# Attention with 16 heads of width 8 on one Trainium2 core: two heads on the two row halves of TensorE, head stacks built through DRAM, maxima six pairs ahead

## The reference, cut to what matters

```python
Q, K, V = relu(xn @ Wq + bq), relu(xn @ Wk + bk), relu(xn @ Wv + bv)   # 16 heads, width 8
scores = Q K^T / sqrt(8)                    # per head, 512 x 512
scores = where(key_mask == 0, NEG, scores)  # key_mask: token's sum is not 0
scores = where(tril == 0, NEG, scores)      # causal
out = (softmax(scores) * query_mask) @ V + xn
s = gamma * (out - mean) / sqrt(var + 1e-8) + beta
x1 = x + s * g                              # g: gate from the feed-forward part
```

## Time and profile before

| | |
|---|---|
| median of 3 runs | 3548.79 us (3545.11 to 3551.12) |
| profiled execution | 3541.39 us |
| its span, first to last instruction | 3539.7 us |
| mean granted TensorE clock over the span | 0.933 |
| attention0, first score matmul of its first unit | 489.0 us |
| attention0, first score matmul of its last unit | 1415.4 us |
| start of attention1's first DMA | 1453.6 us |

### The profile page before, as it was taken

One profiled execution on the slowest core, in us unless ns is written; L12 is line 12 of the kernel. 1 busy time (PEld: TensorE's weight loads), 2 busy tenths in 40 slices (PEclk: granted clock), 3 DMA queues, 4 the chain that ended last, 5 costly groups with the idle time before them and its releaser, 6 DMA issues. The chain is left out here.

```text
span 3539.7 us, 67118 instructions
## 1 busy us (share of the span) xinstructions
PE 2813.7 (79%) x21299; PEld 1950.8 (55%) x21313; DVE 2355.2 (67%) x5836; ACT 1522.0 (43%) x2623; POOL 1306.7 (37%) x1528
## 2 busy tenths in 40 slices
PE   0035348777777777499999999999999986999999
PEld 0023224444444444266666666666666656888888
DVE  8977657777777777366666666666666645555555
ACT  3434325444444445245555555555555542232222
POOL 4557621212121211155555555555555550000000
PEclk9977669998998989699999999999999998999999
DMA  1000021322222221101111111111111102010010
GB/s 48 0 6 0 8 40 35 50 35 46 40 42 37 43 42 32 42 24 35 34 35 36 34 34 34 34 34 34 34 34 34 31 29 69 24 36 24 27 32 24
DMA packets 152526, 116.23 MB, mean 33 GB/s; under 512 B 35506, under 2 KB 127155, under 8 KB 152372
## 3 DMA queue, kind: packets, MB, share of 16 engines
q1 hardware_dynamic: 152372, 114.25, 14.0%
HBM read 60.96 MB, written 17.32 MB: 22 GB/s over the span
## 5 line engine op out<-in xcount | busy, mean ns | idle before, releaser
L1518 DVE CUSTOM_DVE_ANT_0 a_scored<-a_pMax,a_causal 128x128 bf16<-128x128 f32 (+3 forms) x1024 | 449.8, 485 | 446.1 <-PE a_pMax L1642 446.1
L927 DVE TENSOR_REDUCE a_max<-a_pMax 128x2 f32<-128x256 f32 (+3 forms) x512 | 406.9, 823 | 206.7 <-PE a_pMax L1063 198.4
L866 ACT ACTIVATE a_PT<-a_pST 128x512 f32<-128x512 f32 x640 | 370.7, 597 | 401.9 <-PE a_pST L603 264.9
L1435 ACT ACTIVATE a_PT<-a_pST 128x1024 f32<-128x1024 f32 (+1 forms) x384 | 339.2, 883 | 365.4 <-PE a_pST L1632 354.3
L1061 PE MATMUL a_pMax<-a_KS,a_QS 96*128 96x128 bf16 (+3 forms) x1024 | 283.6, 329 | 200.3 <-DMA a_QS<-a_mT 131.3
L1384 POOL TENSOR_SCALAR_AFFINE_SELECT a_PT<-a_PT 128x256 f32<-128x256 f32 x512 | 204.0, 411 | 607.0 <-ACT a_PT L1435 576.6
L1921 ACT ACTIVATE m_silu<-m_pG 128x512 f32<-128x512 f32 x256 | 153.3, 599 | 409.1 <-PE m_pG L2013 409.1
L1650 PE MATMUL a_pO<-a_PT,a_V 128*64 128x512 f32 (+3 forms) x2048 | 307.4, 443 | 0.7 <-POOL a_PT L1384 0.7
L1061 PEld LDWEIGHTS a_pMax<-a_KS,a_QS 96*128 96x128 bf16 x1024 | 107.0, 106 | 305.9 <-issue 195.0
L1074 PE MATMUL a_pST<-a_QS,a_KS 99*128 99x512 bf16 (+3 forms) x1024 | 257.9, 317 | 16.4 <-ACT a_PT L866 14.4
L794 POOL TENSOR_TENSOR a_rest<-a_qk,a_parts 128x512 f32<-128x512 f32 x32 | 37.0, 1157 | 591.2 <-ACT a_parts L859 591.1
(11 more groups left out here) (282 smaller groups left out, 6914.5 us busy)
## 6 DMA issues: line engine op xcount, KB each, us to landing
a_rden<-inverse_sums_dram SPq DMA_DIRECT2D x256, 128.0 KB, 2.9
a_QS<-a_parts SPq DMA_DIRECT2D x192, 64.0 KB
a_KS<-a_parts SPq DMA_DIRECT2D x192, 64.0 KB
a_xn_staged<-xn SPq DMA_DIRECT2D x32, 256.0 KB, 2.4
a_max_rows<-a_mT SPq DMA_DIRECT2D x512, 2.0 KB
ln_x<-in_L_attn_x SPq DMA_DIRECT2D x8, 512.0 KB, 7.2
a_x<-in_L_attn_x SPq DMA_DIRECT2D x16, 256.0 KB, 3.0
x_dram<-a_att SPq DMA_DIRECT2D x16, 256.0 KB, 3.7
```

The costliest lines, as they stand in the source:

```text
L866: a.activation(PT[p][:, k], pST[(5 * p + k) % 2][:], ACT.Exp, scale=SCALE).then_inc(exped.sem, 1)
L927: v.tensor_reduce(MX[:, 2 * p:2 * p + 2, j], pMax[j % 2][:, :, 0:(j + 1) * P], AX.X, ALU.max, negate=True).then_inc(maxed.sem, 1)
L1435: a.activation(PT[s.q % 2][:, :, k * TOK:k * TOK + w], pST[:, :, 0:w], ACT.Exp, scale=SCALE).then_inc(exped.sem, 1)
L1518: last = v.tensor_tensor_reduce(scored[:, cc, at:at + w], pMax[:, cc, at:at + w], causal[:, TOK - w:], -1.0, 3e38, ALU.add, ALU.min, MX[pa ...
```

## The change

attention0 is rewritten.

- Head h (0 to 7) lies on rows 0 to 63, head h+8 on rows 64 to 127 of one QS and one KS tile; a pair is h and h+8. A unit still has four pairs; a batch has two units ("group" 0 and 1) that share the tiles, so there are two QS and two KS tiles, one for each parity of b. Six parts are rows 0 to 47, the key mask row 48, the maxima rows 49 to 51.
- Score and maximum matmuls have 64 (or 49) rows, one on each half, into the two banks of one tile; the mask matmuls keep 128 rows. A pair has three score rounds (512, 384 + 128, 256 columns a head) and three maximum rounds.
- pST is one tile of two banks; each exponential covers both heads (1024, 1024 and 512 elements).
- The parts go to DRAM with three DMAs each for Q and K (`put_q`, `put_k`), two batches ahead, and come back with one DMA for each half and tensor (`stack`), one batch ahead.
- Maxima are made six pairs ahead: two of the pairs of u+1 (its third and fourth) and two of u+2 (its first and second) during unit u. The rows of maxima take two DMAs.
- The bias of V is added by a matmul with one row; ScalarE evacuates all of V with one relu. The mask factor and the mask column are gone (the ninth column is one).
- The order of all engines is written anew; projections of batch b+2 stand in odd units, values of b+1 in even units.

The diff, cut to its core:

```diff
-    MASK, MROW = 64, 96
+    NPART = 6
+    HALF, MASK, MROW = P // 2, NPART * DH, NPART * DH + 1
     VC = DH + 1
-    PER_D, PER_G = 112, 20
-    STACK = 7 * 16
+    PAIRS, NS, NM, LEAD = 4, 3, 3, 6
+    AT = (0, TOK, 2 * TOK, TOK + 3 * P)
+    WIDTH = (TOK, TOK, 2 * P)
+    ROUNDS = (((0, 0),), ((0, 1), (3 * P, 3)), ((0, 2),))
+    MAXB = (((3, 0),), ((0, 0), (2, P)), ((1, 0),))
+    PER_D, FIRST_LESS_D, PER_G = 94, 30, 20
...
-        QS = [sb(f"QS{i}", [P, UH, TOK], BF16) for i in range(4)]
-        KS = [sb(f"KS{i}", [P, UH, TOK], BF16) for i in range(4)]
+        QS = [sb(f"QS{i}", [P, UH, TOK], BF16) for i in range(2)]
+        KS = [sb(f"KS{i}", [P, UH, TOK], BF16) for i in range(2)]
...
-        vtmp = sb("vtmp", [P, TB, P])
-        PT = [sb(f"PT{i}", [P, 5, TOK]) for i in range(4)]
-        MX = sb("max", [P, UH, TB])
-        mrest = sb("mrest", [P, UH * TB])
-        mp = sb("mparts", [P, 3, UH * TB], BF16)
-        mT = sb("mT", [UH * TB, 3, P], BF16)
+        PT = [sb(f"PT{i}", [P, 2, sum(WIDTH)]) for i in range(PAIRS)]
+        MX = sb("max", [P, 2, PAIRS, TB])
...
-        pST = [ps(f"pST{i}", [P, TOK]) for i in range(2)]
+        pST = ps("pST", [P, 2, TOK])
...
+            def lead(self, p, last):
+                ahead = 1 if p < 2 else 2
+                if last and self.s + ahead > 3:
+                    return None
+                return self.u + ahead, (self.s + ahead) % 4, (p + 2) % PAIRS
...
+            def put_parts(dst, n, groups, put):
+                for at, count, k, parts in groups:
+                    src = part[:, n, k:k + 1, :].to_broadcast([P, count, TOK]) if parts == 1 else part[:, n, k:k + count, :]
+                    sp.dma_start(dst[at:at + count].rearrange("a s d h t -> (s d h) a t"), src).then_inc(put, 16)
+            def put_q(b):
+                q_parts.wait(sp, b)
+                if isinstance(b, int) and b == 1:
+                    sp.wait_ge(q_stacked, STACKED_Q)
+                put_parts(qs_d, 0, ((0, 3, 0, 1), (3, 2, 1, 1), (5, 1, 2, 1)), q_put)
...
+            def stack(b, parity, last_score=None):
+                Q, K = QS[parity], KS[parity]
                 row = mask_d[bass.ds(b * TB, TB), :].rearrange("(o a t) p -> o a (t p)", o=1, a=1)
+                sp.wait_ge(q_put, PUT * (b + 1))
+                sp.sem_inc(puts_seen, 1)
+                sp.wait_ge(k_put, PUT * (b + 1))
+                sp.sem_inc(puts_seen, 1)
+                if last_score is not None:
+                    st_ready.wait(sp, last_score)
+                for half in range(2):
+                    sp.dma_start(Q[part_rows(half), :, :], qs_d[:, half].rearrange("a d h t -> a d (h t)")).then_inc(q_stacked, 16)
+                for half in range(2):
+                    sp.dma_start(K[part_rows(half), :, :], ks_d[:, half].rearrange("a d h t -> a d (h t)")).then_inc(k_stacked, 16)
+                    sp.dma_start(K[one_row(half, MASK), :, :], row.to_broadcast([1, UH, TOK])).then_inc(k_stacked, 16)
+            def m_rows(u, parity, group):
                 mT_in.wait(sp, u)
                 for half in range(2):
+                    sp.dma_start(QS[parity][HALF * half + MROW:HALF * half + MROW + 3, PAIRS * group:PAIRS * (group + 1), :],
+                                 mT[3 * PAIRS * TB * half:3 * PAIRS * TB * (half + 1), :]).then_inc(m_put, 16)
...
+                    if not n.odd:
+                        if n.values:
+                            stack(b + 1, 1 - n.parity, NS * PAIRS * u - 1)
+                        if not (last and s == 0) and not (last and s == 2):
+                            stage(b + 2)
+                        if not n.no_before:
+                            load_x(b - 1)
+                    elif not n.no_before:
+                        store_x1(b - 1, 1 - n.parity)
+                    if n.prepare:
+                        put_q(b + 2)
+                    if not n.end:
+                        m_rows(u + 1, (s + 1) % 4 // 2, (s + 1) % 2)
+                    if n.prepare:
+                        put_k(b + 2)
...
+            def v_evac(b, parity):
+                v_ready.wait(a, b)
+                pv_done.wait(a, 4 * (b - 1) - 1)
+                heads = V[parity][:, :, 0:HEADS * VC].rearrange("p t (h d) -> p t h d", d=VC)
+                a.activation(heads[:, :, :, 0:DH], pM[:].rearrange("p (t h d) -> p t h d", t=TB, d=DH), ACT.Relu).then_inc(v_in.sem, 1)
+            def exp(u, p, k):
+                if k == 0:
                     pv_done.wait(a, 2 * (u - 1) + p // 2)
+                st_ready.wait(a, NS * (PAIRS * u + p) + k)
+                at, w = k * TOK, WIDTH[k]
+                a.activation(PT[p][:, :, at:at + w], pST[:, :, 0:w], ACT.Exp, scale=SCALE).then_inc(exped.sem, 1)
...
+                    exp(u, 0, 0)
+                    if n.prepare:
+                        x_in(b + 2)
+                    exp(u, 0, 1)
+                    if not n.start:
                         o_evac(2 * u - 1)
+                    exp(u, 0, 2)
+                    if n.prepare:
+                        q_evac(b + 2)
+                    for k in range(NS):
+                        exp(u, 1, k)
+                    exp(u, 2, 0)
+                    if n.prepare:
+                        k_evac(b + 2)
+                    if n.values:
+                        v_evac(b + 1, 1 - n.parity)
+                    exp(u, 2, 1)
+                    exp(u, 2, 2)
+                    o_evac(2 * u)
+                    if not n.end:
                         m_evac(u + 1)
+                    for k in range(NS):
+                        exp(u, 3, k)
...
-                    step.did(v.tensor_scalar(heads[:, :, 0:DH], vtmp[:, t].rearrange("p (h d) -> p h d", d=DH), 0.0, km,
-                                             ALU.max, ALU.mult))
-                    step.then(v.tensor_copy(heads[:, :, DH], km.to_broadcast([P, HEADS])))
-                v.sem_inc(v_in.sem, 1)
...
+                    lead(0, (0, 1, 2))
+                    lead(1, (0, 1, 2))
+                    if not n.end:
                         m_split(step, u + 1)
+                    if not n.start:
+                        o_normal(step, 2 * u - 1, *((b, 0) if n.odd else (b - 1, 1)), 1, n.parity if n.odd else 1 - n.parity)
+                    lead(2, (0, 1, 2))
+                    if not n.no_before:
+                        if n.odd:
+                            normalise_x1(step, b - 1, 1 - n.parity)
+                        else:
+                            normalise(step, b - 1, 1 - n.parity)
+                    lead(3, (0, 1, 2))
+                    o_normal(step, 2 * u, b, int(n.odd), 0, n.parity)
...
+                    into = pM[:, t * P:(t + 1) * P]
+                    pe.matmul(into, XT[:, t * P:(t + 1) * P], wv[:], start=True, stop=False)
+                    mm = pe.matmul(into, one[0:1, :], rows[0:1, 0, :], start=False, stop=True)
...
+            def max_round(u, par, pair, p, m):
+                n = NM * (PAIRS * u + p) + m
+                bank = pMax[(NM * p + m) % 2]
+                maxed.wait(pe, n - 2)
+                for k, (j, at) in enumerate(MAXB[m]):
+                    w = (j + 1) * P
+                    for half in range(2):
+                        pe.matmul(bank[:, half, at:at + w], QS[par][masked_rows(half), pair, j * P:(j + 1) * P],
+                                  KS[par][masked_rows(half), pair, 0:w], start=(k == 0), stop=False)
+                for half in range(2):
+                    mm = add_far(pe, bank[:, half], [at + j * P for j, at in MAXB[m]], identb, far)
...
+            def score_round(u, par, pair, p, k):
+                exped.wait(pe, NS * (PAIRS * u + p) + k - 1)
+                for at, kb in ROUNDS[k]:
+                    for half in range(2):
+                        rows = split_rows(half)
+                        pe.matmul(pST[:, half, at:at + TOK - kb * P], KS[par][rows, pair, kb * P:(kb + 1) * P],
+                                  QS[par][rows, pair, kb * P:TOK], start=(at == 0), stop=False)
+                for half in range(2):
+                    mm = add_far(pe, pST[:, half], [at for at, _ in ROUNDS[k]], far, identb)
+                mm.then_inc(st_ready.sem, 1)
...
+                    pe.wait_ge(m_put, M_PUT * (u + 1))
+                    score(0, 0)
+                    lead(0, 0)
+                    if n.prepare:
+                        if not n.start:
                             o_in.wait(pe, 2 * u - 2)
+                        turn_x(b + 2)
+                    if not n.start:
+                        weigh(u - 1, 1, 1 - group, par if n.odd else 1 - par)
+                    score(0, 1)
+                    lead(0, 1)
+                    if n.prepare:
+                        project(b + 2, wq, q_ready)
+                    score(0, 2)
+                    lead(0, 2)
+                    score(1, 0)
+                    lead(1, 0)
+                    score(1, 1)
+                    lead(1, 1)
```

(37 more changed lines are left out.)

443 lines of the change are left out of this document (168 added, 275 removed).

## The result

The changed kernel takes 3807.9 us (median; 3806.0 to 3809.1) against 3547.8 us of the kernel before beside it: a ratio of 1.0736 [1.072, 1.0752]. Slower, as forecast, but by 260 us and not by 52, and far out of the range. The profiled executions span 3804.3 and 3539.7 us.

What follows compares the result with a forecast made beforehand. No engine full; TensorE waits for maxima's rows, VectorE for maxima. New chain 53.0 + VectorE's lateness 8.5 + stack load 1.3 = 62.8 us a batch against 59.8; +47, last unit +5: 3601 us, range 3495 to 3690.

Steps and rivals of the forecast that it cites:

- signs of being wrong: Mask matmul following at 0.22 us, TensorE's waits for VectorE below 5, or the stacked Q and K load over 12 us.
- The clock: TensorE in attention0: removing the wait for maxima's rows also gives back some half-clock stretches, at most 4 us a batch.
- rival 2: Load of Q and K parts from DRAM uses six of sixteen engines: 109 GB/s, 4.7 us a batch, 3654 us; chance 0.21.
- Values: TensorE's value matmuls plus four bias matmuls, counted above the exponentials' cover: about 1.8 us a batch.
- the sum: Batch of attention0: 61.5 + 1.3 = 62.8 us against 59.8, +3.0 us, x 15.5 = +47 us.
- Stacks: Q and K parts loaded back from DRAM at 145 GB/s in 11 us; TensorE loses 1.3 us a batch.
- VectorE's waits: TensorE waits for late VectorE work in attention0: 9.6 us together, 8.5 of it uncovered, a batch.
- the ring: Buffer of two maximum rounds between TensorE and VectorE; normalisation makes TensorE wait 2.7 us (even unit), 2.1 (odd).
- The drain: TensorE changing between 64-row and 128-row matmuls: 0.16 us a change, two a round, 24 rounds: 7.7 us a unit.
- rival 3: No cost of changing matmul shape with 2-byte weights: batch 59.0 us, 3541 us, within 0.2% or a little faster; chance 0.10.
- The last unit: Unit without maxima at attention0's end: some 22 us by the new chain against 17, +5 us.
- Rival 1: VectorE keeps up and half-clock stretches vanish: batch 54 to 58 us, kernel 3460 to 3520 us; chance 0.28.

Runs made afterwards that it cites:

- The filler: Changed kernel plus unread matmuls on TensorE ahead of three waits (10, 6 and 28): 3769.1 us, ratio 1.0628.
- the fitted filler: Unread matmuls, 12 before the keys' projection and 8 before the stacks' wait, added to the kernel with four edits and 64 satisfied waits: 3547.2 us.
- mended kernel: Changed kernel with 128-row bias, halves' DRAM layout, late normalisation, mask first in maximum rounds, and 64 satisfied waits at attention1's start: 3606.0 us.
- the pad: Changed kernel plus 64 already satisfied waits at the start of attention1 on TensorE and on VectorE: 3785.4 us, ratio 1.0684.

## Why the prediction was wrong

The direction was right and its mechanism partly so; the size failed by the steps below. A batch was to go from 59.8 to 62.8 us; it went to (1625.89 - 487.68)/15.5 = 73.4, measured between the first score matmuls of unit 0 and of unit 31, as in the earlier trace rows. Of its own signs of being wrong one came true: the stacks' load took over 12 us.

- **The clock, the step that failed.** But for a clause in rival 2, the prediction counted the clock as something that the change could only give back ("some of the half-clock stretches ... 4 us"), and then placed 8.5 us of waits for VectorE and a wait for the stacks in every batch at their own length, all of TensorE's work at full clock. Behind them, in the batch shown, TensorE ran at 1.2 GHz for some microseconds: the granted clock fell to 0.76 where I had taken 1. The weightings alone, 3.78 us in place of 2.36, are 4 x 1.42 = 5.7 us a batch. The filler showed 145 us of busy time from it, the fitted filler 59 us of kernel time from two waits of the mended kernel. How much of the 207 us over the forecast is the clock's alone stays open: the filler gave back 39 us net, with its own work in it.
- **Values, mis-sized:** 1.8 us in the sum; 5.7 measured (875.64 to 881.37). The bias matmul's single row changes TensorE's shape eight times. I had priced changes of shape for the masks and overlooked them here. Of the 3.9 us over the forecast they are about 1.6 (0.42 us a matmul at full clock, 3.4 in all), the clock 2.3. Making the rows 128 gave 66 us.
- **Stacks, mis-sized:** 1.3 us a batch; 7.1 in the batch shown, 3.7 on the mean of 14 waits. Rival 2 named the mechanism and the rate (109 GB/s; measured 98 to 116), but priced no clock behind the wait at that rate. Undoing it gave 48 us.
- **VectorE's waits, right in length:** at the ring 2.7 and 2.1 us late predicted, 2.86 and 2.38 measured; 1.8 before the keys' projection against 1.57; 1.3 before the turning of x against 1.15. In sum TensorE waited 124.3 us for VectorE in the 15.5 batches, 8.0 each, against 8.5. Moving the normalisation gave 44 us, with the half clock behind the ring in it.
- **The drain, there but over-priced:** 0.10 and 0.11 us, not 0.16 each. The mask follows after 0.32 us, between the 0.35 that was to confirm it and the 0.22 that was to refute it; rival 3 is out. With 0.21 a round the 24 rounds of a unit cost 5.0 us and not 7.7, and a batch's 24 score rounds 1.4 us less than in the sum. Taking half of the changes away without delaying ScalarE gave nothing by itself.
- **The last unit:** +5 us forecast; from unit 31's first to its last score matmul 26.0 us against 13.6, +12.4, with weightings of 4.1 us at half clock (the forecast also had the last weighting in it, the measured spans end before it).
- **Attention1:** taken as unchanged; +42 us. With the pad alone it is 35 us shorter in the profile, and with the other edits too it comes within 5 us of the kernel before (1407.0 to 1412.5 against 1407.6).

Added up, 3.9 (values), 2.4 (stacks) and 5.7 (weightings) are 12.0 us a batch over the forecast, and the drain takes 1.4 back, where 10.6 were measured. That the sum closes is in part luck: other work at half clock is not in it (the keys' projection takes 1.10 us a matmul where the queries' takes 0.66), nor is what ScalarE's time covers. Rival 1 is out: it wanted under 5 us of waits for VectorE a batch.

## What to carry to other kernels

Price a new wait of TensorE at its length plus the work behind it at half clock, not at its length alone; when such a wait can't be removed, matmuls that nobody reads and that fit into it can pay (59 us here), and those that don't fit cost their length (96 us here). Look at every matmul of a changed stretch for its number of rows, the little bias ones too, and at the slowest index of every large transfer. If an untouched stage gets slower, count the instruction transfers in its loops before looking for a cause in the data.

## What the runs showed of the hardware that was not expected

- The clock was low behind short waits too. In the kernel after, one of 1.57 us before 838.67 already stood before work at the lower clock (1.00 from 836 to 838 us, 0.62 to 840; the projection took 2.08 us for 1.02), and from 832 to 834 us the clock was 0.50 behind waits of only 0.26 and 0.92 us among sparse rounds. In attention1 of the kernel before, whose work is otherwise full, the waits of 0.75 us on the mean had no such effect: 1.00 in every window from 1743 to 1831 us.
- A matmul with one row between matmuls with 128 costs 0.20 us a change at full clock and 0.29 at half clock; a change between 64 (or 49) and 128 rows about 0.11 us at either.
- The same loop, moved by 64 instructions on two engines, lost 65 instruction transfers and 35 us of 1450.
